# Normalised x by features from a second load and a row of norms through DRAM, with a new order of the PSUM ring

## The reference

```python
normed = gamma * (x / max(norm(x), 1e-12)) * 128 ** 0.5
q, k, v = heads(normed @ w_q) * 16 ** -0.5, heads(normed @ w_kv)   # 8 heads of 16
q, k = taylor2(q), taylor2(k)              # [1, x, all products x_i x_j / sqrt(2)]
state, k_sum = k^T v, sum(k)               # per head, over 512 tokens
att = (q @ state) / max(q @ k_sum, 1e-5)
x1 = layernorm(x + att @ w_out)
h = silu(x1 @ w1 * s1) * (x1 @ w2 * s2)    # 512 wide
h = gelu(h @ h1 * hs1); h = gelu(h @ h2 * hs2)
out = layernorm(x1 + h @ w3 * s3)
```

## Time and profile before

| | |
|---|---|
| median of 3 runs | 576.32 us (576.15 to 576.57) |
| the profiled execution | 576.77 us, of which the trace's span is 575.0 us |
| PE, busy share of the span | 95% |
| PEld | 71% |
| ACT, DVE | 81%, 80% |
| POOL | 29% |
| mean granted TensorE clock | 0.983 of full speed |
| DMA | 12.25 MB, mean 21 GB/s |

### The profile page before, as it was taken

The page is one execution under the profiler, slowest core; times in us unless marked ns, Lnnn a source line. Parts: engine busy times, 40 slices in busy tenths (PEclk is TensorE's granted clock), DMA queues, the critical chain, the costliest instruction groups (busy, mean ns, idle before and its releaser), DMA issues.

```text
span 575.0 us, 11379 instructions
## 1 busy us (share of the span) xinstructions
PE 548.1 (95%) x3598; PEld 408.4 (71%) x3598; DVE 458.6 (80%) x976; ACT 463.2 (81%) x954; POOL 164.4 (29%) x246
## 2 busy tenths in 40 slices
PE   6869999999999999999999999999999999999994
PEld 3445877778687777768777776877777787786672
DVE  4775869878797988879798887979788797968664
ACT  4956797988879788887978888797888879787773
POOL 4541412323151332315133222413322241320000
PEclk9968999999999999999999999999999999999998
DMA  8000000000000000000000000000000000000000
GB/s 285 2 21 1 19 2 17 5 18 20 19 18 18 18 0 18 18 18 18 18 18 3 15 18 18 18 18 18 12 6 18 18 18 19 0 19 1 19 2 36
DMA packets 7366, 12.25 MB, mean 21 GB/s; under 512 B 816, under 2 KB 1840, under 8 KB 7344
## 3 DMA queue, kind: packets, MB, share of 16 engines
q1 hardware_dynamic: 7056, 11.86, 6.0%
q10 hardware_dynamic: 288, 0.10, 0.1%
HBM read 7.77 MB, written 4.19 MB: 21 GB/s over the span
## 4 chain that ended last, share of the span: by engine, by line
PE 69%; ACT 17%; issue 8%; DVE 5%; POOL 1%; DMA 1%; ACTq 0%; DVEq 0%; POOLq 0%
PE fps L422 20%; PE fps L423 20%; PE ring L359 6%; ACT phiT L644 5%; PE ring L389 5%; PE ring L339 4%; PE ring L313 4%; ACT fps L694 3%; ACT hid_hi L693 3%; PE ring L406 3%; PE ring L398 2%; PE ring L320 2%; ACT restq L649 2%; ACT x1T_hi L654 1%; PE fps L462 1%
## 5 line engine op out<-in xcount | busy, mean ns | idle before, releaser
L422 PE MATMUL fps<-hid_hi,w_hi 128*128 128x512 f32 x576 | 228.5, 397 | 2.3 <-DVE hid_lo L917 1.8
L423 PE MATMUL fps<-hid_lo,w_hi 128*128 128x512 f32 x576 | 226.9, 394 | 0.0
L422 PEld LDWEIGHTS fps<-hid_hi,w_hi 128*128 128x128 f32 x576 | 108.3, 188 | 29.3 <-DVE hid_lo L917 6.4
L693 ACT ACTIVATE hid_hi<-fps,col 128x512 fp32r<-128x512 f32 x128 | 90.5, 707 | 46.3 <-PE fps L423 45.9
L423 PEld LDWEIGHTS fps<-hid_lo,w_hi 128*128 128x128 f32 x576 | 108.4, 188 | 21.5
L917 DVE TENSOR_TENSOR hid_lo<-fps,hid_hi 128x512 fp32r<-128x512 f32 x128 | 88.1, 689 | 28.9 <-ACT fps L694 25.9
L644 ACT ACTIVATE phiT<-ring 128x512 f32<-128x512 f32 x128 | 78.6, 635 | 16.4 <-PE ring L339 16.2
L903 DVE SCALAR_TENSOR_TENSOR h<-fps,col,gate_zo 128x512 f32<-128x512 f32 x64 | 47.9, 748 | 49.8 <-ACT gate_zo L680 43.7
L694 ACT ACTIVATE fps<-fps,col 128x512 f32<-128x512 f32 x128 | 86.9, 679 | 0.0
L249 DVE TENSOR_TENSOR phi_k<-phi_k 128x896 f32<-128x896 f32 x64 | 73.0, 1145 | 1.4 <-ACT v_one L617 1.3
L339 PE MATMUL ring<-qT,sel 128*128 128x512 f32 x128 | 55.3, 441 | 7.7 <-ACT phiT L644 4.4
(11 more groups left out here) (98 smaller groups left out, 921.3 us busy)
## 6 DMA issues: line engine op xcount, KB each, us to landing
x_b<-in_x SPq DMA_DIRECT2D x16, 256.0 KB, 2.5
out<-gate_zo SPq DMA_DIRECT2D x16, 256.0 KB, 2.0
w_raw<-in_h SPq DMA_DIRECT2D x2, 1024.0 KB, 8.4
w_raw<-in_w SPq DMA_DIRECT2D x3, 256.0 KB, 4.0
sel_raw<-in_sel SPq DMA_DIRECT2D x1, 320.0 KB, 4.8
w_qkv_raw<-in_w_kv SPq DMA_DIRECT2D x1, 128.0 KB, 2.9
const<-in_consts ACTq DMA_DIRECT2D x1, 92.0 KB, 3.2
w_qkv_raw<-in_w_q SPq DMA_DIRECT2D x1, 64.0 KB, 2.9
```

Source lines behind the costliest of these rows:

```text
L422: nc.tensor.matmul(fps[:, bank, :], w_hi[:, o:o + P], hi, start=start, stop=False)
L423: return nc.tensor.matmul(fps[:, bank, :], w_hi[:, o:o + P], lo, start=False, stop=stop)
L693: nc.scalar.activation(hid[1 - layer][0][:, m, :], fps[:, bank, :], ACT.Gelu, scale=scale)
```

## The change

Three things are changed together.

**x by features.** The host passes x a second time, transposed (`xT`, features by tokens). SP loads it into `x_cols` (256 KB per item). The norms `rn` (128 x 4) are written by SP to a DRAM row of 512 floats, `rn_rows`, with four DMAs of 128 single floats, and, when these have landed, read back with one DMA that gives all 128 partitions the same row (`rn_row`, 256 KB). POOL then makes `xnT_hi`, `x_scaled` and `xnT_lo` with three 128x512 operations (`normed_cols`). For items 1 to 15 the transposes of x on PE, the copy on ACT and the subtraction on DVE are gone; item 0 keeps them. The first projection now waits for POOL's last operation (`x_lo_ready`).

**Order.** `RING` has no `xT`, and other banks and another order: `kv2` and `kv3` stand earlier, `qT` before `out`, `sq6` before `state`. The lists of PE, ACT and DVE follow.

**Fill.** Step 2's feed-forward part starts before the last sums and the state of item 1; DVE does one tile of sums and one more weight rounding; the loads of SP are in another order. Also, the first matmul of a hidden layer's input tile waits for its hi part alone (`gelu_hi_ready`, `hi_ready`), and only the second one for the lo part.

```diff
 RING = (
-    ("stateT", MIDDLE, 0), ("restT", MIDDLE, 1), ("xT", FRONT, 2), ("acc0", MIDDLE, 0), ("acc1", MIDDLE, 1),
-    ("kv0", FRONT, 3), ("kv1", FRONT, 2), ("kv2", FRONT, 3), ("out", MIDDLE, 0), ("qT", FRONT, 1), ("kv3", FRONT, 2),
-    ("sq0", FRONT, 3), ("sq1", FRONT, 0), ("rest0", FRONT, 2), ("sq2", FRONT, 1), ("sq3", FRONT, 3), ("sq4", FRONT, 0),
-    ("rest1", FRONT, 2), ("sq5", FRONT, 0), ("state", FRONT, 1), ("sq6", FRONT, 3), ("sq7", FRONT, 2))
+    ("stateT", MIDDLE, 0), ("restT", MIDDLE, 1), ("acc0", MIDDLE, 0), ("acc1", MIDDLE, 1),
+    ("kv0", FRONT, 3), ("kv1", FRONT, 2), ("kv2", FRONT, 3), ("kv3", FRONT, 2), ("qT", FRONT, 0), ("out", MIDDLE, 1),
+    ("sq0", FRONT, 2), ("sq1", FRONT, 1), ("rest0", FRONT, 3), ("sq2", FRONT, 0), ("sq3", FRONT, 2), ("sq4", FRONT, 1),
+    ("rest1", FRONT, 3), ("sq5", FRONT, 0), ("sq6", FRONT, 2), ("state", FRONT, 1), ("sq7", FRONT, 3))
...
+    rn_d = [bass.AP(rn_rows.tensor, rn_rows.offset + j * P, [[1, P], [1, 1]]) for j in range(NT)]
+    rn_all = bass.AP(rn_rows.tensor, rn_rows.offset, [[0, P], [1, N]])
...
+            def spread_norms(n):
+
+                sp.wait_ge(rn_ready, n + 1)
+                for j in range(NT):
+                    sp.dma_start(rn_d[j], rn[:, j:j + 1]).then_inc(rn_stored, 16)
+                sp.wait_ge(rn_stored, 16 * NT * n)
+                sp.dma_start(rn_row[:, :], rn_all).then_inc(rn_row_loaded, 16)
...
+                    if is_positive(t):
+                        sp.wait_ge(x_scaled_ready, t)
+                    sp.dma_start(x_cols[:, :], xT[bass.ds(t + 1, 1)].rearrange("b d n -> (b d) n"))\
+                        .then_inc(cols_loaded, 16)
+                    spread_norms(t + 1)
...
             def project_kv(t, j):
                 if j == 0:
-                    pe.wait_ge(ring_free[bank_of(RING, "xT")], read(RING, t, "xT"))
+                    pe.wait_ge(x_lo_ready, t + 1)
...
+            def normed_cols(t):
+
+                pool.wait_ge(cols_loaded, 16 * t)
+                pool.wait_ge(rn_row_loaded, 16 * t)
+                pool.wait_ge(ring_full, written(RING, t - 1, "qT"))
+                nc.gpsimd.tensor_tensor(xnT_hi[:, :], x_cols[:, :], rn_row[:, :], ALU.mult).then_inc(x_hi_ready, 1)
+                nc.gpsimd.tensor_tensor(x_scaled[:, :], x_cols[:, :], rn_row[:, :], ALU.mult).then_inc(x_scaled_ready, 1)
+                pool.wait_ge(x_scaled_ready, t)
+                pool.wait_ge(x_hi_ready, t + 1)
+                nc.gpsimd.tensor_tensor(xnT_lo[:, :], x_scaled[:, :], xnT_hi[:, :].bitcast(F32), ALU.subtract)\
+                    .then_inc(x_lo_ready, 1)
...
                 if middle:
                     spread_rest(t)
+                if front and not is_step(t, 0):
+                    normed_cols(t)
                 if front:
                     k_small(t, 0)
...
-                if front and not is_step(t, B - 1):
-                    normed_x(t + 1, 1 - par)
+                if front and not is_step(t, 0) and not is_step(t, B - 1):
+                    norm_of_x(t + 1)
...
+            normed_cols(1)
             spread_rest(1)
             k_small(1, 0)
...
             def second_step():
                 transpose_state(1)
                 transpose_rest(1)
-                transpose_x(1)
                 apply_main(1)
                 apply_rest(1)
-                project_kv(1, 0)
-                project_kv(1, 1)
+                for j in range(NT):
+                    project_kv(1, j)
+                project_q(1)
+                pe.wait_ge(w_out_loaded, 16)
+                project_out(1)
+                sums_of_q(1, 0)
+                sums_of_q(1, 1)
+                rest_of_q(1, 0)
                 pe.wait_ge(lo_sums_ready, 3)
                 nc.tensor.matmul(fps[0:1, 3, 0:3], half_c, lo_sums[:, :], start=True, stop=True)\
                     .then_inc(lo_sums_added, 1)
...
+                sums_of_q(1, 2)
...
                     if ffn:
                         layer1(t, 0, in_full)
+                    if is_step(t, 2):
+                        sums_of_q(1, 3)
+                        sums_of_q(1, 4)
+                    if ffn:
                         layer1(t, 1, in_full)
                     if is_step(t, 2):
+                        rest_of_q(1, 1)
+                        sums_of_q(1, 5)
+                        sums_of_q(1, 6)
                         state(1)
-                        sums_of_q(1, 6)
                         sums_of_q(1, 7)
...
                     if front:
-                        transpose_x(t)
+                    if is_step(t, 0):
+                        transpose_x0()
```

More of the change, by code:

```diff
@@ L134, in build @@
         rn = sb("rn", [P, NT])
+        rn_row = sb("rn_row", [P, N])
+        x_cols = sb("x_cols", [P, N])
+        x_scaled = sb("x_scaled", [P, N])
         xn = sb("xn", [P, NT, D])
@@ L278, in _ @@
             sp.dma_start(sel_raw[:, :], sel_d).then_inc(sel_loaded, 16)
-            peeled(step, 0)
+            sp.dma_start(x_b[1][:, :, :], x_d[1]).then_inc(x_loaded[1], 16)
+            sp.dma_start(x_cols[:, :], xT[1]).then_inc(cols_loaded, 16)
             load_ffn_weights(1, (oh1, h1t))
+            spread_norms(1)
             load_ffn_weights(2, (oh2, h2t))
@@ L380, in apply_main @@
                 pe.wait_ge(ring_free[bank_of(RING, "stateT")], read(RING, t, "stateT"))
+                if is_step(t, 1):
+                    pe.wait_ge(ring_free[bank_of(RING, "sq6")], read(RING, 0, "sq6"))
                 for g in range(2):
@@ L415, in transpose_x1, with product @@
                 mm.then_inc(f_full, 1)
-            def product(bank, o, hi, lo, start, stop, in_full):
+            def product(bank, o, hi, lo, start, stop, in_full, wait_lo=None):
+                w = w_raw if in_full else w_hi
                 if in_full:
-                    nc.tensor.matmul(fps[:, bank, :], w_raw[:, o:o + P], hi.bitcast(F32), start=start, stop=False)
-                    return nc.tensor.matmul(fps[:, bank, :], w_raw[:, o:o + P], lo.bitcast(F32), start=False, stop=stop)
-                nc.tensor.matmul(fps[:, bank, :], w_hi[:, o:o + P], hi, start=start, stop=False)
-                return nc.tensor.matmul(fps[:, bank, :], w_hi[:, o:o + P], lo, start=False, stop=stop)
+                    hi, lo = hi.bitcast(F32), lo.bitcast(F32)
+                nc.tensor.matmul(fps[:, bank, :], w[:, o:o + P], hi, start=start, stop=False)
+                if wait_lo is not None:
+                    pe.wait_ge(*wait_lo)
+                return nc.tensor.matmul(fps[:, bank, :], w[:, o:o + P], lo, start=False, stop=stop)
             def layer1(t, m, in_full):
@@ L711, in step @@
                 if middle:
-                    square_sums(t - 1, 7, 6)
-                if ffn:
+                    square_sums(t - 1, 7)
+                if ffn and not is_step(t, 2):
                     silu(t, 1)
@@ L752, in step @@
                 if is_step(t, 1):
-                    a, b = w_parts[0]
-                    nc.scalar.activation(w_hi[:, a:b], w_raw[:, a:b], ACT.Copy).then_inc(w_hi_ready[0], 1)
+                    weights_low_bits(2, 1)
+                if ffn:
+                    gelu(t, 0, 0)
+                    gelu(t, 0, 1)
+                if front and not is_step(t, 0):
+                    copy_q(t)
+                if is_step(t, 1):
+                    weights_low_bits(0, 2)
+                if ffn:
+                    gelu(t, 0, 2)
+                    gelu(t, 0, 3)
                 if front:
-                    square_sums(t, 0)
+                    square_sums(t, 0, 1)
                 if ffn:
```

203 lines of the change are left out of this document (100 added, 103 removed).

## The result

The changed kernel takes **724.8 us** (723.9 to 725.5), against 576.5 us of the kernel before, run beside it: ratio 1.257, 95% interval 1.254 to 1.259. The profiled execution has a span of 723.1 us where before had 575.0, and a mean granted clock of 0.887. The prediction said 581.0 and at most 600; it is wrong by 144 us, and outside its range.

The account below looks back on a forecast made before the run. PE's own instructions, plus one 0.30 us wait per step, were taken as the bound. Profiled 576.77 us, less 10.9 freed, plus 15.6 for a new wait (13 x 1.2), gave 581.5, or 581.0 against the median; range 566 to 600.

Parts of the forecast that it names:

- Any new wait on PE that is longer than what the change frees makes the kernel slower.: On PE, said to have no slack: a new wait slows the kernel, with break-even at 0.84 us a step.
- Transposes and sq5, -4.9 and -3.9: PE's steps: four transposes go, 0.35 us in 14 steps (-4.9); sq5's wait for its bank goes, 0.30 in 13 (-3.9).
- Tail, -0.6: Kernel's end: PE's hi matmul may run ahead of a lo part in three places, hiding 0.23 us each; 0 to -1.8.
- Fill, -1.5, between -4 and +2: Kernel's start: the first FFN matmul may start 2.5 us earlier, against a later transpose_rest(1); taken as -1.5 us.
- It lands ... I take 2.0: Chain from norms to projection: the last small write of norms lands 2.0 us after issue, bounds 1.3 to 3.1.
- The row, 2.5: Chain from norms to projection: reading the row of norms to 128 partitions takes 2.5 us, like the load of x.
- Three operations of POOL at 1.04, and 0.9 of contention: Before the projection: three POOL operations take 3.1 us, plus one hold of 0.9 by VectorE's gate_lo, bounds 0 to 2.5.
- named it for a sign: Sign of a wrong forecast: POOL's 512-element product with two full inputs is not 1.04 us.
- Rival B: Full contention: all three POOL operations wait once for VectorE, 2.0 us instead of 0.9; s = 2.3, 595 us; chance 0.12.
- The clock: PE's clock: a wait of 2 us in each step could halve it, costing up to 2 us more per step.
- rival C: Slow small stores or a colder clock: both landings take 3.1 us, s = 2.9, 603 us; chance 0.08.
- s = 4.5: Upper bound of PE's wait per step before the first projection: both landings 3.1 us, contention 2.5; forecast was 1.2.

Follow-up runs that it names:

- e8: e1 with POOL's three operations on all 512 columns for item 1 alone, 8 columns for later items; 579.7 us.
- e9: e1 with one wait, for the low half, ahead of each pair of matmuls, as in the kernel before; 595.4 us.
- e14: The kernel before with only the split wait added: first matmul waits for the high half, the second for the low; 575.2 us, ratio 0.997.
- e3: The changed kernel with the norms written by one DMA of 128 pieces of 16 bytes, in another order; 594.1 us.
- e12: The changed kernel with the 512 floats written to DRAM 64 bytes apart by four DMAs, and the row read from xT; 595.8 us.
- e13: The changed kernel with only the first 128 norms written, side by side in one DMA, and the row read from xT; 693.7 us.
- e2b: The changed kernel with the four writes of norms put into one DMA of 512 floats to the same places; 721.4 us.
- e4: The changed kernel with the single floats written into one partition of SBUF, and the row read from 128 rows of xT; 629.2 us.
- e1: The changed kernel with norms written and read for item 1 alone, later items scaled with that row; 592.2 us, ratio 1.026.
- e5: The changed kernel with norms made and written two items ahead, the row read a step after the writes; 592.0 us, ratio 1.027.
- e11: e5 with item 1 transposed on PE in the fill, POOL's part cut to one operation, moved to the end of the step before; 573.1 us, ratio 0.993.

## Why the prediction was wrong

- **"Any new wait on PE that is longer than what the change frees makes the kernel slower."** Right, and it decided the sign.
- **Transposes and sq5, -4.9 and -3.9.** Right: 0.87 a step in e8 against 0.65. The wait at sq5 is gone. Of the 0.22 more, 0.1 are PE's waits on `hid_lo` (1.6 us in 400 before, 0.5 in e8). The rest may be the later wait for the low half (0.27 in e9, but 0.03 in e14) or POOL's `xn`, which left the step's end; no run separates these.
- **Tail, -0.6.** -1.2, of which the later wait is 0.9 (e14 and e9). Three times 0.23 would have been 0.7.
- **Fill, -1.5, between -4 and +2.** Wrong: +18.2, and 8.0 more in step 2, which this term also held. The place was named (`spread_rest(1)` behind `normed_cols(1)`, "at worst some 2.5 us"), but its size was one landing of the row. It has the four writes in it too, and so took 10.4. The same chain had been priced a few lines on for the steady step, and was not carried back here.
- **"It lands ... I take 2.0": the step that failed.** About 7.0. The prediction said that no row shows a DMA of single floats, and still bounded it by rows of other DMAs, 1.3 to 3.1. Those rows, a store of 256 KB and a load of 9 KB at the start, do not have its small pieces side by side in DRAM. e3 and e12 show that the landing depends on how the pieces lie in memory, and no row of that kind was in the trace of before. By 13 steps, 4.9 us are 64 us.
- **The row, 2.5.** 4.2 to POOL's start, where 2.6 was taken. In the kernels whose row came behind small writes side by side (e13, e3, after and e2b) it landed in 4.0 to 4.8, behind others (e4, e12) in 2.8. e12 and e13 read the same bytes, so it is not what is read. The cause stays open; 1.6 x 13 = 21 us.
- **Three operations of POOL at 1.04, and 0.9 of contention.** 1.26 each; 1.04 was the price with a broadcast operand, as the prediction had named it for a sign. There was no contention in the changed kernel, since POOL now works while PE and VectorE stand idle: `hid_lo<-h` is at 686 ns (the row below). So the sum of the two, 4.0 against 4.2, was right by luck. Where POOL does meet VectorE at that place, in e3, POOL is held for 1.0 us in all, near the 0.9 that was taken. But VectorE is late there too, and in e1, where PE never waits for POOL's last operation, the meeting costs 0.83 a step all the same. Rival B said that "DVE would be held too" and took it for nothing.

```profile
L940 DVE TENSOR_TENSOR hid_lo<-h,hid_hi 128x512 fp32r<-128x512 f32 x64 | 43.9, 686 | 10.6 <-ACT hid_hi L714 9.1
```

- **The clock.** Named in rival C for a wait of 2 us, at up to 2 more. With 7.9 us of wait the step is 42.95 - 32.57 - 7.9 = 2.5 longer still, if e8 is the step without both; 32 us in all. The stretches above agree: from 295.2 to about 300.6 PE ran at half the clock, and so lost some 2.7. In e3 a wait of 1.4 us left the clock at 1.00 in every stretch of 4 us from 260 to 312, and the step is 32.57 + 1.3 + 0.3 for everything else. In e4 it fell, behind a wait of 2.6 (length, PE busy, PEclk, DMA share, GB/s; e3, then e4):

```profile
268.00:272.00 4.00, 2.62 (x17) 1.00 0.00 0
272.00:276.00 4.00, 4.00 (x22) 1.00 0.00 0
```

```profile
284.00:288.00 4.00, 1.62 (x7) 0.83 0.00 0
288.00:292.00 4.00, 4.00 (x17) 0.75 0.00 0
```

- **Rival C** was the mechanism, "slow small stores" with the colder clock, priced at 603 and given 0.08. Its price was tied to the same upper bound of 3.1. The prediction's own largest wait, s = 4.5, would have been 565.4 + 13 x 4.5 = 624, above the 600 of its range, and the 724.8 lies above that too: the bound of the landing was the fault, not only the chance.

Summed: 13 steps were to grow by 13 x (1.2 - 0.65) = 7 us. They grew by 123: 13 x 7.9 of wait and 13 x 2.5 of clock, less 13 x 0.87. The fill and step 2 grew by 26 where they were to shrink by 1.5.

## What to carry to other kernels

Price a transfer by a row with the same piece size, the same distance between pieces and the same target; where there is none, leave the upper end open, above all when its completion stands in a chain that repeats each step. Write many small values in pieces of 16 bytes (e3), or put the round trip a step ahead of its use, since the distance of one step hid it whole (e5). Work that is moved to POOL is not free because POOL is idle: count the VectorE operations beside it that stretched here, those on two SBUF operands (e1, e3) and the layer norm's 128x128 scalings (e11), and what waits for them.
